# Perceiver block on one Trainium2 core: the first unit of weights loaded in two column halves, and key rotations moved ahead of weight turns

## The reference

```python
x = x + cross_attention(layernorm(x), ctx)     # q: 32 heads of 128 from wq1 (4096 x 1024), k, v: 8 heads, RMS norms, out wo1
x = x + self_attention(layernorm(x))           # 32 heads of 32, 8 kv heads, rotary embedding on q and k, causal, out wo2
x = x + mixing(layernorm(x))                   # softmax and 50 Sinkhorn iterations on 4 x 4 matrices per token, branch of 256 x 256
```

## Time and profile before

| | |
|---|---|
| median of 3 runs | 1177.3 us (1177.2 to 1181.17) |
| profiled execution, its own time | 1179.86 us |
| its span, first to last instruction | 1178.1 us |
| TensorE busy | 1080.6 us, 92% |
| VectorE busy | 819.2 us, 70% |
| ScalarE busy | 478.5 us, 41% |
| chain that ended last | PE 77%, DVE 18%, ACT 2% |
| mean granted TensorE clock | 0.972 |

### The profile page before, as it was taken

One profiled execution on the slowest core, in us unless ns is written; L12 is line 12 of the kernel. 1 busy time (PEld: TensorE's weight loads), 2 busy tenths in 40 slices (PEclk: granted clock), 3 DMA queues, 4 the chain that ended last, 5 costly groups with the idle time before them and its releaser, 6 DMA issues.

```text
span 1178.1 us, 17695 instructions
## 1 busy us (share of the span) xinstructions
PE 1080.6 (92%) x6392; PEld 904.2 (77%) x6392; DVE 819.2 (70%) x1867; ACT 478.5 (41%) x989; POOL 155.0 (13%) x161
## 2 busy tenths in 40 slices
PE   3999999999999999999999999999998988896555
PEld 2888888888888887888888887888886767785444
DVE  4744445567678868767778786475566899835998
ACT  3432323444545446544545555241323234312333
POOL 0000000332233212333323310000000000001000
PEclk9999999999999999999999999999998999997777
DMA  9595657234443332344444214899537031000001
GB/s 226 134 204 119 153 131 164 65 90 104 103 106 69 69 71 68 87 101 94 100 101 98 49 45 90 173 219 241 99 79 136 19 49 25 4 11 1 1 1 71
DMA packets 161692, 111.11 MB, mean 94 GB/s; under 512 B 73161, under 2 KB 153673, under 8 KB 161633
## 3 DMA queue, kind: packets, MB, share of 16 engines
q1 hardware_dynamic: 160576, 109.29, 42.7%
q10 hardware_dynamic: 1056, 1.05, 0.4%
HBM read 90.91 MB, written 18.87 MB: 93 GB/s over the span
## 4 chain that ended last, share of the span: by engine, by line
PE 77%; DVE 18%; ACT 2%; issue 1%; DMA 1%; SPq 0%; DVEq 0%; POOL 0%; ACTq 0%
PE ps L519 28%; PE ps L465 28%; PE ps L850 7%; PE ps L451 5%; PE ps L530 4%; PE ps L547 3%; DVE wt L1362 2%; DMA raw<-in_L_xattn_q_proj_w 1%; DVE xr L1997 1%; DVE small L1880 1%; DVE small L1904 1%; DVE small L1884 1%; DVE small L1877 1%; DVE small L1901 1%; DVE small L1895 1%
## 5 line engine op out<-in xcount | busy, mean ns | idle before, releaser
L519 PE MATMUL ps<-wt,act 128*128 128x512 f32 x1536 | 389.1, 396 | 0.0
L465 PE MATMUL ps<-wt,act 128*128 128x512 f32 x1440 | 332.8, 393 | 9.7 <-DVE wt L1362 9.7
L465 PEld LDWEIGHTS ps<-wt,act 128*128 128x128 f32 x1440 | 272.1, 190 | 68.1 <-DVE act L1346 7.7
L519 PEld LDWEIGHTS ps<-wt,act 128*128 128x128 f32 x1536 | 275.9, 188 | 49.4
L1362 DVE TENSOR_TENSOR wt<-raw,wt 128x512 fp32r<-128x512 f32 x192 | 120.1, 684 | 85.7 <-ACT wt L953 85.7
L953 ACT ACTIVATE wt<-raw 128x512 fp32r<-128x512 f32 x192 | 106.4, 622 | 97.6 <-DVE raw L1354 52.8
L1354 DVE STREAM_TRANSPOSE raw<-raw 128x1024 f32<-128x1024 f32 x96 | 112.8, 1219 | 37.7 <-DMA raw<-in_L_xattn_o_proj_w 21.6
L1346 DVE TENSOR_TENSOR act<-ps,act 128x512 fp32r<-128x512 f32 x112 | 75.8, 684 | 87.0 <-ACT act L948 87.0
L850 PE MATMUL ps<-wt,act 128*128 128x512 f32 x480 | 124.8, 409 | 6.0 <-DVE spare L1674 5.1
L948 ACT ACTIVATE act<-ps 128x512 fp32r<-128x512 f32 x112 | 65.9, 596 | 123.5 <-PE ps L451 123.2
L850 PEld LDWEIGHTS ps<-wt,act 128*128 128x128 f32 x480 | 89.7, 194 | 25.1 <-issue 7.0
(11 more groups left out here) (144 smaller groups left out, 1094.4 us busy)
## 6 DMA issues: line engine op xcount, KB each, us to landing
xr<-in_ctx SPq DMA_DIRECT2D x64, 256.0 KB, 6.0
raw<-in_L_xattn_o_proj_w SPq DMA_DIRECT2D x32, 512.0 KB, 14.2
raw<-in_L_xattn_q_proj_w SPq DMA_DIRECT2D x30, 512.0 KB, 9.2
q_rows<-G SPq DMA_DIRECT2D x64, 128.0 KB, 3.5
xr<-q_rows SPq DMA_DIRECT2D x16, 512.0 KB
ot_hi<-spare SPq DMA_DIRECT2D x64, 128.0 KB, 2.7
act<-ot_hi SPq DMA_DIRECT2D x32, 256.0 KB, 9.3
raw<-in_L_xattn_k_proj_w SPq DMA_DIRECT2D x8, 512.0 KB, 9.5
```

Of the source, the lines that this page charges most:

```text
L465: mm = pe.matmul(banks[t], lhs(p == 2, c, t), wt[:, n_slot, int(p == 1), c, :], start=(acc_from and q == 0), stop=(acc_to and q == 3 * NC ...
L519: mm = pe.matmul(bank, src[int(p == 2)][:, c, kt * P:(kt + 1) * P], wt[:, slot, int(p == 1), c, :], start=(q == 0), stop=(q == 3 * NC - 1))
```

## The change

The change has two parts. (Its short description also names alternating chains in the tail. The diff has no line there; in both kernels the two Sinkhorn chains already take turns.)

**Start.** Unit 0 is loaded in eight pieces of 128 columns (256 KB, runs of 512 B): the first four hold chunks 0 to 3 and count on a new semaphore, the others chunks 4 to 7. SyncE issues x tile 0, two first-half pieces, x tile 1, two second-half pieces; ScalarE issues `ident`, two first-half pieces, two second-half pieces. VectorE turns and splits the first half before it does stats of tile 1; each group of layernorm low halves has its own place. TensorE waits for the low halves of a tile by group, and turns tiles 2 and 3 after matmul 18 of the tile before.

**Unit 20.** VectorE's turns of unit 21 are mixed with the low halves of layernorm tiles 2 and 3 and the key rotations; ScalarE's high halves of unit 21 come between the high halves of layernorm tiles and ahead of `copy_key`.

```diff
+        first_half = sem("first_half")
+        def first_unit(half):
+            to = raws[0].rearrange("p (b e) -> p b e", b=16)
+            return [(to[32 * a:32 * a + 32, :, 128 * half:128 * half + 128],
+                     wq1[0:UW, 256 * a + 128 * half:256 * a + 128 * half + 128].rearrange("(b p) e -> p b e", p=32))
+                    for a in range(4)]
...
             sp.dma_start(xr[:, 0, :], x_rows[:, 0, :]).then_inc(x_loaded[0], 16)
+            for dst, rows in first_unit(0)[0:2]:
+                sp.dma_start(dst, rows).then_inc(first_half, 16)
             sp.dma_start(xr[:, 1, :], x_rows[:, 1, :]).then_inc(x_loaded[1], 16)
-            sp.dma_start(ident[:], ident_in).then_inc(ident_ready, 16)
-            for dst, rows in unit_pieces(0)[0:2]:
+            for dst, rows in first_unit(1)[0:2]:
                 sp.dma_start(dst, rows).then_inc(raw_loaded[0], 16)
...
-            def ln_ready(t):
-                pe.wait_ge(lo_done, 2 * t + 2)
+            def ln_ready(t, c):
+                if c % 4 == 0:
+                    pe.wait_ge(lo_done, 2 * t + c // 4 + 1)
...
-            query_unit(0, 0, ln_ready, next_ln, chunks=True)
+            query_unit(0, 0, lambda t: None, next_ln, chunks=True, arrived=ln_ready, at={1: 17, 2: 17})
...
-            for dst, rows in unit_pieces(0)[2:4]:
+            sc.dma_start(ident[:], ident_in).then_inc(ident_ready, 16)
+            for dst, rows in first_unit(0)[2:4]:
+                sc.dma_start(dst, rows).then_inc(first_half, 16)
+            for dst, rows in first_unit(1)[2:4]:
                 sc.dma_start(dst, rows).then_inc(raw_loaded[0], 16)
             normalise(0)
             hi_ln(0, 0, T)
-            for c in (0, 1):
+            for c in range(4):
                 hi_w(0, 0, c)
             normalise(1)
-            for c in (2, 3):
-                hi_w(0, 0, c)
-            hi_ln(0, 1, T)
             for c in range(4, NC):
                 hi_w(0, 0, c)
+            hi_ln(0, 1, T)
...
+            sc.wait_ge(acc_done, 64)
+            for c in (0, 1):
+                hi_w(21, 1, c)
             hi_ln(M_LN2, 2, T2)
+            for c in (2, 3):
+                hi_w(21, 1, c)
             hi_ln(M_LN2, 3, T2)
+            for c in (4, 5, 6, 7):
+                hi_w(21, 1, c)
...
-            ln_lo(M_LN2, 2, T2)
-            ln_lo(M_LN2, 3, T2)
...
             turn_unit(21, 0)
             turn_unit(21, 1)
+            ln_lo(M_LN2, 2, T2)
             rotate_keys(0)
             turn_unit(21, 2)
-            turn_unit(21, 3)
-            lo_unit(21, 0)
-            lo_unit(21, 1)
+            ln_lo(M_LN2, 3, T2)
             rotate_keys(1)
-            for c in (2, 3, 4):
+            turn_unit(21, 3)
+            for c in (0, 1):
                 lo_unit(21, c)
             rotate_keys(2)
-            for c in (5, 6, 7):
+            for c in (2, 3, 4, 5):
                 lo_unit(21, c)
             rotate_keys(3)
+            for c in (6, 7):
+                lo_unit(21, c)
```

More of the change, by code:

```diff
@@ L454, in products @@
             def products(n, n_slot, banks, lhs, before, acc_from=True, acc_to=True, between=None, chunks=False,
-                         arrived=None):
+                         arrived=None, at=None):
                 for t in range(NT):
@@ L466, in products @@
                                        start=(acc_from and q == 0), stop=(acc_to and q == 3 * NC - 1))
-                        if q == 11 and between:
+                        if q == (at or {}).get(t, 11) and between:
                             between(2 * t)
@@ L481, in _, with query_unit @@
             pe.wait_ge(ident_ready, 16)
-            def query_unit(n, par, before=None, between=None, chunks=False):
+            def query_unit(n, par, before=None, between=None, chunks=False, arrived=None, at=None):
                 if not chunks:
@@ L490, in acc_ready @@
                         pe.wait_ge(acc_free, 4 * n - 3 + t)
-                products(n, par, acc, lhs_of(0), before or acc_ready, between=between, chunks=chunks)
+                products(n, par, acc, lhs_of(0), before or acc_ready, between=between, chunks=chunks,
+                         arrived=arrived, at=at)
             pe.wait_ge(ln_done, 1)
             turn_ln(0, T, 0)
-            def ln_ready(t):
-                pe.wait_ge(lo_done, 2 * t + 2)
+            def ln_ready(t, c):
+                if c % 4 == 0:
+                    pe.wait_ge(lo_done, 2 * t + c // 4 + 1)
             def next_ln(k):
@@ L969, in _ @@
             hi_ln(0, 0, T)
-            for c in (0, 1):
+            for c in range(4):
                 hi_w(0, 0, c)
             normalise(1)
-            for c in (2, 3):
+            for c in range(4, NC):
                 hi_w(0, 0, c)
             hi_ln(0, 1, T)
-            for c in range(4, NC):
-                hi_w(0, 0, c)
             normalise(2)
@@ L1206, in hi_out2 @@
                 sc.activation(o2_dst(0, k), four(ps[:, 7, :]), ACT.Copy).then_inc(o2_hi, 1)
-            sc.wait_ge(acc_done, 64)
-            for c in range(NC):
-                hi_w(21, 1, c)
             for t in range(NT):
@@ L1390, in first_stats, with turn_first, ln_lo_half @@
                 stats(t)
-            first_stats(0)
-            first_stats(1)
[L1394 to L1405, removed]
+            def turn_first(j):
+                if j == 0:
+                    v.wait_ge(first_half, 64)
+                if j == 2:
+                    v.wait_ge(raw_loaded[0], raw_count[0])
+                y = raw_chunks(0, 2 * j, 2)
+                v.transpose(y, y).then_inc(w_turned, 1)
+            def ln_lo_half(t, g):
+                lo(2 * t + g, g, ln_dst(1, t, g), ln_dst(0, t, g), bank=T)
+            first_stats(0)
+            turn_first(0)
+            turn_first(1)
+            ln_lo_half(0, 0)
+            for c in range(4):
+                lo_unit(0, c)
+            first_stats(1)
+            turn_first(2)
+            turn_first(3)
+            ln_lo_half(0, 1)
+            for c in range(4, NC):
+                lo_unit(0, c)
+            ln_lo_half(1, 0)
             first_stats(2)
-            lo_unit(0, 6)
-            lo_unit(0, 7)
+            ln_lo_half(1, 1)
             first_stats(3)
@@ L1739, in _ @@
             turn_unit(21, 1)
+            ln_lo(M_LN2, 2, T2)
             rotate_keys(0)
             turn_unit(21, 2)
+            ln_lo(M_LN2, 3, T2)
+            rotate_keys(1)
             turn_unit(21, 3)
-            lo_unit(21, 0)
-            lo_unit(21, 1)
-            rotate_keys(1)
-            for c in (2, 3, 4):
+            for c in (0, 1):
                 lo_unit(21, c)
             rotate_keys(2)
-            for c in (5, 6, 7):
+            for c in (2, 3, 4, 5):
                 lo_unit(21, c)
             rotate_keys(3)
+            for c in (6, 7):
+                lo_unit(21, c)
             for j in range(4):
```

## The result

The changed kernel takes 1164.22 us (median of four, 1163.21 to 1164.86) against 1179.24 us for the kernel before on the same chips: ratio 0.9868, 95% interval 0.9838 to 0.9899. Its profiled execution takes 1164.21 us, 15.7 us less than that of before.

A forecast was written before the change was run, and what follows sets the result against it. TensorE, busy 1080.6 of 1178.1 us, loses time waiting for the first load and unit 20's key rotation, with slow clock after. Gains of 8.3 + 6.0 = 14.3 us from 1177.3 give 1163.0 us, range 1159.5 to 1171.

The forecast's parts named there:

- Landing of the first half: Start, unit 0: the first half's load, split over SyncE's and ScalarE's queues, lands at 10.3 us.
- the bound of 11.8: Start: latest landing of the first half, with both queues' 1 MB at 156 GB/s instead of 210.
- Packets of 512 B: Unit 0's load: smaller packets move 200 GB/s; with doubled pieces the whole unit lands at 18.0 us instead of 17.03.
- The estimate from the Trainium skill: Unit 0's load: cutting 512 KB pieces to 256 KB costs 0.3 us each, some 2.4 us for the unit.
- Chunk 4 at 21.8 us: Start: after the second half lands at 18.0 us, TensorE goes on at 21.8 instead of 29.16, 7.4 us earlier.
- Slow clock: 24 matmuls from chunk 4: about half of 1.86 us of slow clock and waits is won, 0.9 us.
- Part 1: Start: loading the first unit in two halves gains 8.3 us, bounds 4.9 and 9.3.
- Part 2: Units 20 and 21: key rotations ahead of turns bring the first query 6.0 us earlier, bounds 5.0 and 7.4.
- the new wait: Unit 21: TensorE waits 0.8 us for chunk 6's low half, which stands behind the last key rotation.
- the 0.5 us of cover: Unit 21: ScalarE's high halves and copies end at 911.7 us, wanted at 912.2, so hidden by 0.5 us.
- the rival that had it so: After either gain: DMA issues, low clock or VectorE's chain give one back, 1166 us (1169 with two); chance 0.10.
- The packet rival: Start: 512 B packets cost as much time as 1 KB ones, second half at 26.7 us, total 1171; chance 0.12.

The follow-up runs named there:

- three_on_sync: Changed kernel with three of the four first-half pieces on SyncE's queue and one on ScalarE's; 1166.95 us, ratio 0.9896.
- first_alone: Changed kernel with three first-half pieces and then all second-half pieces on SyncE's queue, ScalarE issuing only ident and one first-half piece; 1165.16 us, ratio 0.9855.
- uncut: Changed kernel with unit 0 loaded in four 256-column pieces (1 KB packets), both SyncE pieces ahead of x tile 1; 1171.33 us, ratio 0.9926.
- one_wait: Changed kernel with VectorE's first turn of unit 0 waiting for both halves, loads and orders kept; 1169.42 us, ratio 0.9923.
- start_only: Changed kernel with VectorE's and ScalarE's order at units 20 and 21 put back as before; 1172.67 us, ratio 0.9940.
- unit20_only: Kernel before with only the new VectorE and ScalarE order at units 20 and 21; 1174.79 us, ratio 0.9956.

## Why the prediction was right, by its steps

The forecast was 1163.0 us and 14.3 us gained; measured were 1164.22 and 15.0 (medians), 15.7 between the profiles. The forecast started from 1177.3 us, the median of three runs; with the fourth it is 1179.24, and that is why the time came out above the forecast although more was gained. Both mechanisms were right. Where a size agrees, it is in part luck, as follows.

- **Landing of the first half.** 10.3 us forecast, 11.43 measured, inside the bound of 11.8. Mis-sized for a reason the working left out: it put the half in the place of x tile 1 on SyncE's queue and let ScalarE's share be "not the later one". It was the later one. three_on_sync and first_alone show that the second-half pieces moving at the same time are the cause; without them the half landed at 9.55 and 10.19 us.
- **Packets of 512 B.** Priced at about 1 us for the unit (18.0 against 17.03). Measured is 0.2 to 0.7 us against the old start and 1.8 against uncut, which differs in its queues too; the price alone is open, and 1 us lies between. The estimate from the Trainium skill ("DMA: Bandwidth & Descriptors", Bandwidth) was 2.4 us for the unit, from its table of sizes, which is for DMAs issued from GpSimd, not from SyncE and ScalarE as here. No comparison here is as large. What its rule would have advised, not to cut, is not borne out, since uncut is 4.2 us later.
- **Chunk 4 at 21.8 us.** Measured 22.07 (22.02 to 22.42 in the six profiles), but for another reason: not the second half's landing (16.9 at the latest, 18.0 forecast) but VectorE's chain from the late first half, with stats of tile 1 in it. The first half was forecast 1.1 us too early, the second at least 1.1 us too late, and the two errors cancelled. That the time agreed here is luck.
- **Slow clock.** Half of 1.86 us of slow clock and waits was taken; all of it came, since after 22.07 no matmul was slow. The step is the 0.9 us term, mis-sized by 1.0. The first 12 matmuls took 4.36 us, not 5.8, but TensorE then waited 1.23 us for normalise of tile 1, so that gained nothing; nor did the wait cost clock. Even where all 12 were slow (5.42 to 5.46 us in one_wait, uncut and first_alone) the 30 behind them took 7.06 to 7.09 us.
- **Part 1** is 9.2 us against 8.3, within 4.9 to 9.3: 7.1 at chunk 4 (7.4 forecast), 1.9 behind it (0.9), 0.2 on the way to unit 19. Over all profiles of the two starts it is 8.2 to 9.2.
- **Part 2.** 6.6 us against 6.0. The wait and its slow matmuls went and the new wait came (0.65 us, 0.8 forecast), as worked out. Of the 0.6 us that the query is earlier than forecast, 0.4 is TensorE's way from the turn of tile 3 to `turn_key(0)`: 3.64 us (892.60 to 896.24), where 901.80 to 905.8 had been worked out. How much the clock gives back varies: against start_only part 2 is 5.7 us. The two turns in the idle time were free; ScalarE's reordering counted for nothing up to the query, as the 0.5 us of cover said it might.
- **Nothing else moved.** From the end of unit 0 to unit 19 the distance is kept within 0.2 us, so nothing of part 1 was given back, against the rival that had it so. Behind the query 1.8 us were lost and 1.7 gained; the sum of nothing is luck, within the spread of that stretch. With unit20_only's 247.5 us there the changed kernel would have come out 4 us slower. The packet rival (second half at 26.7 us) is excluded by the landing before 16.9 us.

## What to carry to other kernels

When a stream starts on a load, cut it so that the first consumer's share lands first, and then look at what else is under way beside it: leaving the second half off the other queue brought the first matmul 1.2 to 2.2 us forward (13.24 and 13.87 against 15.08 to 15.48). And compare loads only with the same bytes in the same order ahead of them; here two comparisons put the price of cutting at 0.2 and at 1.8 us. On an engine that works in order, an instruction that waits for a round trip through other engines belongs behind whatever frees a buffer; one line moved made 4.7 us. Read such effects at landmarks in the trace where the whole time spreads by more than they are worth.

## What was not expected of the hardware

TensorE's first 12 matmuls of 128 x 512, all of the same program, took 4.33 to 5.46 us in the changed kernel and its variants (4.36 and 4.67 in the two profiles of the changed one), so by their pace the clock rose at different points in them. The granted clock of the window from 12 us reads 1.00 all the same. Unit 0 in 1 KB packets beside x tiles moved up to 347 GB/s in 4 us, against 210 for 1 KB packets alone. And behind the first query the granted clock falls at different places from kernel to kernel, in a stretch that takes 94.5 to 99.4 us; in the kernel before it hardly fell there at all.
